# Message-passing layer: three of eight groups routed, GpSimd and SyncE programs written out, one VectorE add for both strips

## The reference

```
h   = x @ W_in2f
Wij = ssp(f_ij @ W_filt1 + b_filt1) @ W_filt2 + b_filt2     # ssp(v) = softplus(v) - ln 2
Wij = Wij * rcut_ij[:, None]
agg = segment_sum(h[idx_j] * Wij, idx_i)
out = ssp(agg @ W_out1 + b_out1) @ W_out2 + b_out2
return layernorm(x + out)
```

## Time and profile before

| | |
|---|---|
| median of 3 runs | 2207.99 us (2207.87 to 2208.26) |
| the profiled execution | 2206.78 us, its span 2205.0 us |
| TensorE granted clock | 0.977 on average, 1.00 from 170 us on to the end of the groups |
| busy: PE, VectorE, ScalarE, GpSimd | 2078.3, 2014.0, 1646.8, 1600.0 us |
| place of the groups | from about 107 us to 2118 us of the span |

### The profile page before, as it was taken

The page is one execution under the profiler, slowest core; times in us unless marked ns, Lnnn a source line. Parts: engine busy times, 40 slices in busy tenths (PEclk is TensorE's granted clock), DMA queues, the critical chain, the costliest instruction groups (busy, mean ns, idle before and its releaser), DMA issues.

```text
span 2205.0 us, 56243 instructions
## 1 busy us (share of the span) xinstructions
PE 2078.3 (94%) x16913; PEld 1745.7 (79%) x16913; DVE 2014.0 (91%) x4147; ACT 1646.8 (75%) x3972; POOL 1600.0 (73%) x998
## 2 busy tenths in 40 slices
PE   2589999999999999999999999999999999999946
PEld 2468888888888888888888888888888888888833
DVE  6679999999999999999999999999999999999847
ACT  0288878878787878788787887887887877878617
POOL 2058777777777777777777877777777777877754
PEclk8689999999999999999999999999999999999979
DMA  9556555565656565665665565655566565656485
GB/s 325 192 95 101 92 91 95 93 98 93 92 93 99 86 99 92 92 95 92 98 93 92 93 99 86 99 92 92 94 93 98 93 92 92 100 86 95 53 206 142
DMA packets 339397, 231.66 MB, mean 105 GB/s; under 512 B 85319, under 2 KB 318386, under 8 KB 338938
## 3 DMA queue, kind: packets, MB, share of 16 engines
q0 software_dynamic: 135216, 61.60, 30.5%
q1 hardware_dynamic: 193446, 150.03, 26.8%
q10 hardware_dynamic: 10476, 16.77, 2.0%
HBM read 144.67 MB, written 83.58 MB: 104 GB/s over the span
## 4 chain that ended last, share of the span: by engine, by line
PE 85%; DVE 6%; issue 3%; DMA 2%; ACT 2%; POOL 0%; SPq 0%; DVEq 0%; ACTq 0%; POOLq 0%
PE unit_psum L1918 24%; PE unit_psum L1937 22%; PE both_psum L1875 15%; PE total_psum L1888 10%; PE pre_psum L1856 8%; PE both_psum L1900 4%; PE both_psum L1871 2%; DMA src_g<-in_src 1%; DVE scat_hot L1435 1%; DMA h_parts<-h_out 1%; ACT out_rows L1119 1%; DMA table<-total,index 1%; DVE hidden L1353 1%; DVE rank_part L1261 0%; DVE rank L1267 0%
## 5 line engine op out<-in xcount | busy, mean ns | idle before, releaser
L722 POOL DMA_INDIRECT table<-total,index x939 | 1541.3, 1641 | 538.0 <-issue 280.8
L1918 PE MATMUL unit_psum<-moving,route_hot 128*128 128x258 f32 x4368 | 700.6, 297 | 0.8 <-DVE acc_t L1452 0.3
L1918 PEld LDWEIGHTS unit_psum<-moving,route_hot 128*128 128x128 f32 x4368 | 567.9, 190 | 62.1 <-issue 57.7
L904 ACT ACTIVATE ring<-unit_psum 128x258 fp32r<-128x258 f32 x1092 | 423.7, 391 | 203.1 <-PE unit_psum L1918 185.7
L880 ACT ACTIVATE h_dst<-both_psum,cols 128x128 f32<-128x128 f32 x1564 | 445.8, 373 | 150.2 <-PE both_psum L1900 143.2
L1937 PE MATMUL unit_psum<-scat_hot,ring 64*128 64x448 f32 x4368 | 499.9, 373 | 12.0 <-DVE scat_hot L1435 11.0
L1435 DVE TENSOR_SCALAR scat_hot<-node_iota,ring 128x448 fp32r<-128x448 uint16 x1092 | 492.4, 472 | 3.6 <-ACT ring L904 3.3
L1937 PEld LDWEIGHTS unit_psum<-scat_hot,ring 64*128 64x128 f32 x4368 | 399.9, 185 | 114.8 <-ACT ring L904 57.5
L1418 DVE TENSOR_SCALAR route_hot<-node_iota,cols 128x896 fp32r<-128x896 uint16 x624 | 433.9, 723 | 48.7 <-PE unit_psum L1918 48.6
L1875 PE MATMUL both_psum<-w_f,hidden 128*128 128x128 f32 x3128 | 416.5, 276 | 0.0
L1875 PEld LDWEIGHTS both_psum<-w_f,hidden 128*128 128x128 f32 x3128 | 399.8, 193 | 5.2
(11 more groups left out here) (126 smaller groups left out, 1518.7 us busy)
## 6 DMA issues: line engine op xcount, KB each, us to landing
dst_b<-dst SPq DMA_DIRECT2D x391, 128.0 KB
src_b<-src SPq DMA_DIRECT2D x235, 128.0 KB, 3.2
f_t<-in_f_t SPq DMA_DIRECT2D x100, 256.0 KB, 3.2
table<-total,index POOLq DMA_INDIRECT x939
table<-zeros ACTq DMA_DIRECT2D x20, 640.0 KB, 10.0
window<-h_parts SPq DMA_DIRECT2D x391, 32.0 KB
parts<-table SPq DMA_DIRECT2D x48, 256.0 KB, 5.0
h_parts<-h_out SPq DMA_DIRECT2D x12, 384.0 KB, 2.9
```

The costliest lines, as they stand in the source:

```text
L722: pool.indirect_dma_start(tables[table], bass.IndirectOffsetOnAxis(index[:, i, k:k + 1], 0), total[:, i, k, 0:DIM], None, compute_op=ALU.a ...
L904: act.activation(ring[:, r[1] % RING, k, :], unit_psum[:, k % 2, 0:MOVING], ACT.Copy).then_inc(ring_done, 1)
L1918: last = pe.matmul(unit_psum[:, k % 2, 0:MOVING], route_hot[:, tile, k * P:(k + 1) * P], moving[:, tile, :], start=(tile == 0), stop=(tile ...
```

## The change

The share of routed groups is 3 in 8 (places 1, 4, 6 of a period of 8) in place of 8 in 20: 48 periods and 2 more in the last 7 groups make 146 routed groups and 245 plain ones. The orders of PE, VectorE and ScalarE are new ones, for periods of 8. GpSimd and SyncE run the same steps in the same order of groups as before, with no hardware loop and no register arithmetic. The two `add_slice` of a slot sum become one `add_slices` over 2x448 columns, and both first tiles of the next `route` wait for it. The copies to `cols` and the waits for them go; the operations read `edge_cols` and a new `slot_cols` directly. `place_routed` works on 584 columns.

```
-ROUTED_AT = (1, 3, 6, 8, 11, 13, 16, 18)
-LAST_ROUTED = (381, 383, 386, 388)
+PERIOD = 8
+ROUTED_AT = (1, 4, 6)
+LAST_PERIOD = 384
+LAST_ROUTED = (385, 388)
+ROUTE_GROUPS = tuple(g for g in range(LAST_PERIOD) if g % PERIOD in ROUTED_AT) + LAST_ROUTED
...
+        def run_periods(unit, rest):
+            for g in range(-PERIOD, LAST_PERIOD, PERIOD):
+                unit((0, g))
+            rest()
...
             with pool.If(is_narrow):
-                run_groups(pool, step_narrow)
+                run_single(step_narrow)
...
-            def add_slice(m, strip):
+            def add_slices(m):
...
-                b = STRIPS * slot_tile(m) + strip
-                nodes = acc_t[:, b * BUCKET:(b + 1) * BUCKET]
-                dve.tensor_tensor(nodes, nodes, unit_psum[:, strip, 0:BUCKET], ALU.add).then_inc(acc_done, 1)
+                b = STRIPS * slot_tile(m)
+                nodes = acc_t[:, b * BUCKET:(b + STRIPS) * BUCKET].rearrange("p (s n) -> p s n", s=STRIPS)
+                dve.tensor_tensor(nodes, nodes, unit_psum[:, :, 0:BUCKET], ALU.add).then_inc(acc_done, 1)
...
                 elif first_taken(m) is not None:
-                    pe.wait_ge(acc_done, through_adds(m, k))
+                    pe.wait_ge(acc_done, through_adds(m))
```

More of the change, by code:

```diff
@@ L77 @@
 assert BUCKETS * BUCKET == NODE_ROWS > NODES and RING == SLOT_TILES and UNIT % 4 == 0
-assert LAST_UNIT < GROUPS and len(LAST_ROUTED) == FIRST_ROUTED == sum(i < HALF for i in ROUTED_AT)
+assert LAST_UNIT < GROUPS and LAST_PERIOD % PERIOD == 0 == PERIOD % 2 and TABLES == TILES
 assert ROUTES % 2 == 0 and META_HALF * TILES <= GROUP and UNIT % BUSY == 0
@@ L151, in through_half @@
     return 2 * g[0] + g[1] // HALF + 1
-def table_adds(k, adds):
-    return (adds - k + TABLES - 1) // TABLES
-def unit_adds(g, kind, tile):
-    return TILES * sum(kind(i) for i in range(g[1] // UNIT * UNIT, g[1])) + tile
-def table_of(g, kind, tile):
-    return unit_adds(g, kind, tile) % TABLES
 def adds_before(g, kind, tile, k):
-    per_unit = table_adds(k, TILES * sum(map(kind, range(UNIT))))
-    return 16 * per_unit * g[0] + 16 * (g[1] // UNIT * per_unit + table_adds(k, unit_adds(g, kind, tile)))
+    return 16 * (through(g, kind) - 1) + 16 * (k < tile)
 def tiles_in(g):
@@ L233, in through_taken @@
     before = sum(taken((0, n), y) is not None for n in range(m[1]) for y in range(RING))
-    return RING * PER_UNIT * m[0] + (before + sum(taken((0, m[1]), y) is not None for y in range(x + 1)))
+    return before + sum(taken((0, m[1]), y) is not None for y in range(x + 1))
 def first_taken(m):
@@ L465, in build, with columns_of @@
         filter_psum, gather_psum = both_psum[:, 0, :], both_psum[:, 1, :]
+        def columns_of(g, kind):
+            return edge_cols[:, g[1] // HALF, :] if kind is plain else cols[:, g[1] // HALF % 2, :]
         block = ctx.enter_context(nc.Block())
@@ L829, in columns @@
                     act.wait_ge(message_done, through(g0))
-                    if kind is plain:
-                        act.wait_ge(pick_done, through(g0))
-                    if kind is plain:
-                        act.wait_ge(route_hot_done, through(g0, routed))
                 act.activation(cols[:, half % 2, :], edge_cols[:, bass.ds(2 * g[0] + half, 1), :].rearrange("p a c -> p (a c)"),
@@ L873, in weigh_h_dst @@
                     act.wait_ge(h_sum_step, 2 * through(g))
-                act.wait_ge(cols_done, through_half(g))
+                if kind is not plain:
+                    act.wait_ge(cols_done, through_half(g))
                 done_with(act, message_done, g, every, 2)
@@ L1413, in route_one_hot @@
                     dve.wait_ge(route_mm_done, through_tile(plus(r, -1), SLOT_TILES - 1))
-                dve.wait_ge(cols_done, through_half(group_of(r)))
-                place = r[1] % PER_UNIT
-                half = place >= FIRST_ROUTED
-                column = SLOT_COL + (place - FIRST_ROUTED * half) * TILES + tile
-                hot = dve.tensor_scalar(route_hot[:, tile, :], node_iota[:, :], cols[:, half, column:column + 1], None,
+                column = r[1] * TILES + tile
+                hot = dve.tensor_scalar(route_hot[:, tile, :], node_iota[:, :], slot_cols[:, column:column + 1], None,
                                         ALU.is_equal)
@@ L1519, in unit @@
-                compare_src(g(9), plain); compare_src(g(10), plain)
+                add_slices(m(1))
+                multiply(g(4), plain)
+                finish_hidden(pair(3))
+                mark_repeated(g(3), plain)
+                compare_src(g(7), plain); compare_src(g(8), plain)
+                slot_one_hot(m(2), 2)
+                make_index(g(3), plain)
+                compare_dst(g(8))
+                slot_one_hot(m(2), 3); slot_one_hot(m(2), 4)
+                compare_src(g(10), plain)
@@ new lines, in unit @@
+                multiply(g(5), plain)
+                route_one_hot(r(1), 0); route_one_hot(r(1), 1)
+                slot_one_hot(m(2), 5)
+                split_lo(r(1))
+                slot_one_hot(m(2), 6)
+                compare_dst(g(9))
+                multiply(g(6), plain)
+                finish_hidden(pair(4))
+                slot_one_hot(m(3), 0)
+                route_one_hot(r(1), 2)
+                slot_one_hot(m(3), 1)
+                add_slices(m(2))
+                route_one_hot(r(1), 3)
```

798 lines of the change are left out of this document (223 added, 575 removed).

## The result

The changed kernel takes **2369.77 us** (median of four runs, 2353.46 to 2378.63) beside 2207.93 us before: a ratio of 1.0725, 95% interval 1.0666 to 1.0783. The forecast was 2154 us. The profiled execution has a span of 2367.6 us.

A forecast was written before the change was run, and what follows sets the result against it. TensorE was taken to set the pace. Terms: -56.5 (ten groups), -2 (head), -0.5 (drained slot sums at the end), +5 (merged add) = -54 us, taking the median from 2208.0 to 2154 us; range 2144 to 2163.

The forecast's parts named there:

- SyncE's loads stand ahead of need. Zero.: SyncE's loads, with its program written out: issued before they are needed, so zero, at most 2 us either way.
- The third rival: First route tile after each slot sum waits for the whole merged add; at 0.6 us a place 2235 us; chance 0.09.
- TensorE's clock at 1.00: TensorE in the stretch from 1000 to 1200 us: read as busy all 200 us at clock 1.00.
- 56.5 us for ten groups: TensorE: ten groups turned from routed to plain save 5.65 us each, 56.5 us in all, 55 to 59.
- The merged add, +5 us: First route tile after a slot sum: one of three places misses by about 0.1 us, 5 us over 48 periods.
- GpSimd, cost nothing: GpSimd's queue of 20 indirect DMAs a period: 38.8 of 39.3 us, so costed at nothing.
- the 1.665 that I gave as the limit: GpSimd's DMAs: average may grow from 1641 ns to 1.665 us before GpSimd takes over the pace; thinnest margin.
- The rival on GpSimd's pace: GpSimd's DMAs at an average of 1.70 us make a period 40.0 us: 2183 us (2163 to 2200); chance 0.13.
- Written out GpSimd and SyncE, zero: GpSimd's and SyncE's programs without loops or register arithmetic: zero gain, at most 2 us either way.
- The head, -2 us: `place_routed` ahead of the groups, 27 VectorE operations on 584 columns for 624: 2 us less.
- VectorE's exclusive lock: Port pair shared by VectorE and GpSimd: one-hots do not shut GpSimd's DMAs out, measured 1.64 us against 2.9 if they did.

The follow-up runs named there:

- e1: Changed kernel with the source compares of places 2, 3 and 5 moved later on VectorE: 2220.43 us, ratio 1.0055.
- e2: Changed kernel with SyncE issuing each source load ahead of the window load, VectorE's order untouched: 2247.05 us, ratio 1.0167.
- e15: e6 with the source compare of place 5 alone put back to the end of the period: 2277.47 us, ratio 1.0323.
- e13: Kernel before with slot one-hots of half width, which leaves VectorE work out: 2202.85 us, a period of 40.37 us.
- e14: e12 with the route one-hots halved as well: 2166.77 us, a period of 39.65 us.
- e5: e1 with the merged add split again into one add for each strip: 2204.08 us, ratio 0.9979.
- e6: e1 with the merged add kept and two moves in VectorE's order around it: 2195.80 us, ratio 0.9944.
- e4: Kernel before with the two adds of a slot sum merged into one, at the place of the second: 2255.80 us, ratio 1.0217.
- e7: e1 with both the two VectorE moves of e6 and the split adds of e5: 2207.84 us, ratio 0.9996.
- e16: e9 with 64 of 128 rows for each accumulating GpSimd DMA: 2183.83 us, ratio 0.9877.
- e3: Kernel before with GpSimd's and SyncE's programs written out and nothing else: 2206.66 us, ratio 0.9991.
- e9: e6 with the source compares of places 2 and 3 moved into the next period, where VectorE had waited: 2194.33 us, ratio 0.9930.
- e12: e9 with slot one-hots of half width: 2171.09 us, a period of 39.75 us.
- e17: e14 with the GpSimd DMAs halved to 64 of 128 rows as well: 2164.87 us, ratio 0.9802.

## Why the prediction was wrong

In one line of times: 2154 forecast, 2165 TensorE's own list, 2194 with GpSimd and VectorE in the best order run, 2220 with the changed kernel's order at the merged add, 2370 with its source compares ahead of their loads.

- **"SyncE's loads stand ahead of need. Zero."** This step failed, and it is 149 of the 216 us. SyncE issues the load as soon behind the gather as before (0.56 us at place 2, 0.68 before), though at place 2 it takes 1 us longer to land; the row was wanted some 8 us earlier. I read which instructions the new order moves on TensorE and at the add, and did not follow `compare_src`, which it moved too, to its load. What stands ahead of the load in SyncE's list (the window, which waits for the gather of four groups back, and at place 5 the features, which wait for the first layer) stood in the code that was in front of me. Undone on VectorE's side (e1) and on SyncE's (e2), put back (e15): shown. No rival had it. The third rival had the right form, one wait at one place that decides and the kernel slower (2235), but at the add.
- **TensorE's clock at 1.00.** Not a term of the sum at all; 34 us of the miss in the middle are the clock, which fell behind 17 of TensorE's stands. They go with the stands and are part of the 149.
- **56.5 us for ten groups.** Mis-sized. With VectorE and GpSimd out of the way the period is 39.64 where the kernel before (e13) has 40.37, 0.73 us for 0.2 of a routed group: 3.6 us a group, not 5.65. That is 20 us of the sum; 2165 lies only 11 above the forecast, since it is also without VectorE's small waits of the kernel before (5 us, e13) and without the 5 us for the merged add. Both of my prices sum the matmuls that leave and take the spacing of those that stay as fixed. It is not: from start to start a route matmul has 137.6 ns before and 139.9 in e14, one of the second layer 106.9 and 109.6, a gather 59.3 and 60.2, one of the first layer 135.1 and 138.2; over a period that gives back 0.4 us (a matmul of the repeated sum goes the other way, 112.4 to 110.3 ns, and is counted in it). What in the new neighbours makes them so was not tried.
- **The merged add, +5 us.** Mechanism right, size wrong: 16 us in the changed kernel by the split (e5) and 25 by two moves on VectorE (e6), three to five times the term, and 47.6 us in the kernel before's order (e4). In the better order its sign turns: there the merged add is 12 us faster than two (e6 and e7). The term counted only VectorE's work behind the end of the slot sums. In e1 the add began 0.6, 0.04 and 1.2 us behind their end at the three slot sums of a period, since VectorE, some 93% full, was still at earlier work at two of them; the earlier trace rows showed an add that VectorE had been waiting for and were the wrong rows for a busy period.
- **GpSimd, cost nothing.** In the changed kernel right, since the period was so long. In the versions that come near the forecast it is not: 1.690 us a DMA is above the 1.665 that I gave as the limit, and it costs 10.5 us (e16). The rival on GpSimd's pace was thus about a third of what stood between 2165 and 2194; that e16 took 2183.83 us, near the rival's 2183, is chance. That this margin was the thinnest was right as long as the loads were not looked at.
- **Written out GpSimd and SyncE, zero**: right (e3). **The head, -2 us**: right (0.77 for 0.81 us a step; the first message of e9 stands at 118.4 us, before at 120.0).
- **VectorE's exclusive lock**: that a DMA is not shut out was right, though my sentence left out a condition. The Trainium skill, "SBUF — State Buffer" ("Who interferes with whom"), has the lock for VectorE operations in a two-port mode, or with two inputs from SBUF; that the one-hots are such operations is not shown here. In the kernel before, the 150 of 720 DMAs whose first 1.5 us lie for 1.2 us or more under a one-hot take 1.66 us on average, the others 1.64. e13 adds that less VectorE work leaves it at 1.647 us. Why it is 1.611 in e12 and 1.690 in e9 is open.

## What to carry to other kernels

When an order is changed, take every operation that moved, each on its own, and ask what releases it and when that was issued: a consumer can overrun a producer whose program has not changed. In an in-order list of loads, look at every entry ahead of the one that you need, not only at its neighbour. A price for work that leaves an engine holds for its instructions alone; the rest of the list does not keep its spacing. And whether one merged operation or two is better depends on whether its consumer or its own engine is late at that place, so it is to be measured in the order in which it will stand.

## What the runs showed of the hardware

A stand of TensorE of 1.9 us was followed by some 3.5 us at half clock, which costs almost as much as the stand itself; of 62 stands of over 1 us in the changed kernel 17 were followed so, and others as long were not. And halving the rows of an accumulating indirect DMA saves little; all DMAs of e9 (128 rows) and of e17 (64 rows), shortest, median and longest in ns:

```profile
L714 POOL DMA_INDIRECT table<-total,index x756: 1538/1604/2450, 344.3 to 1861.0; - x189
```

```profile
L715 POOL DMA_INDIRECT table<-total,index x765: 1415/1421/1911, 346.6 to 1861.2; - x192
```

The shortest falls from 1538 to 1415 ns (1414 in e16, whose one-hots are full as in e9). If the other 64 rows cost as much again, five sixths of its time on GpSimd do not depend on the rows (an estimate from these two).
